# Row maxima in a rotation of three PSUM banks, one output accumulator for the first image, and a new order within a step

## The chip, the cores and the metric

One core of a Trainium2 chip runs the whole kernel. The metric is the device time in microseconds (us); lower is better. The engines are called as the profile calls them: PE (TensorE, its matmuls; PEld its weight loads), DVE (VectorE), ACT (ScalarE), POOL (GpSimd), SP (the engine that issues most DMAs).

## What is computed

The input is two images `x [2, 128, 32, 32]` in float32. Cut to what matters here, the reference does:

```python
# layer 0, per image: group norm, then 4-head attention over the 1024 pixels
qkv = einsum('bchw,oc->bohw', group_norm(x), qkv_weight)      # head_dim 32
attn = softmax(einsum('bnchw,bncyx->bnhwyx', q, k) / sqrt(C)) # 1024 x 1024 per head
x = einsum('bchw,oc->bohw', einsum('bnhwyx,bncyx->bnchw', attn, v), out_weight) + out_bias + x
# layer 1, on tokens [2, 1024, 128]
t = t + linear_attention(layer_norm(t))          # 8 heads, softmax of keys over the tokens
t = t + top2_of_8_experts(layer_norm(t))         # router, gelu MLP 128 -> 512 -> 128
```

The change is in the softmax attention of layer 0. Its softmax is taken with the true row maximum, so the kernel computes every score twice: once with queries on partitions, to get the maximum of each row, and once transposed (keys on partitions), with the maximum folded into the matmul as two more rows of the contraction, to be exponentiated and multiplied with the values.

## The kernel before

**Tiling.** The attention is cut into 4 units (`UNITS`, u): image u // 2, head pair u % 2. A unit has 16 steps (`STEPS`): two halves of the queries (512 each) by 8 key tiles of 128 (`KT`). That makes 64 steps s. A step's `scores` are two matmuls (one per head, L845) into the banks 2, 3 or 4, 5, alternating by step; ACT exponentiates both at once into `probs` (`exps`, L558); `values` (L864) multiplies with the values and with ones, four products that run beside each other in the four column groups of the array, each issued as two passes, eight matmul instructions a step. They accumulate in bank 6 or 7 (`bank(6 + o % 2)`), where o counts the eight query halves of all units; the accumulator of one o is complete after 8 steps. DVE then closes it: `norm_sums` (a transpose of the row sums), `norm_reciprocal`, `norm_product`, which writes `attn` and frees the bank (`o_used`).

**Row maxima.** One "slot" g is the maximum of 128 query rows of one head over all 1024 keys. Up to g = 7 these are plain. Every later pair slot is "folded": with K1, K2 the two halves of the keys, max(qK1, qK2) = qK2 + relu(q(K1 - K2)). So `max_first(g)` (L806) writes q(K1 - K2) into bank 1, ACT applies relu into the SBUF buffer `above` (`max_above`, L551, two buffers), `max_second(g)` (L826) writes qK2 into bank 0, and DVE adds the two and takes the maximum in one instruction (`max_slot`, L1189). After 8 slots of a group k, DVE makes two columns `mhl` of the 16 maxima; a "rows" slot turns them on PE (L821), DVE copies them to `mrow` (L1181), and SP sends them by DMA into the score operands `Qs` (`max_rows`, L352). `scores` of the first step of a query half waits for that DMA (`mrow_in[k]`). The slots are handed out ahead of the scores: `new_slots(s)` gives steps 0 to 31 two slots each (steps 15 and 31 one); the rows slots fall on steps 5, 9, 14, 19, 23, 28 and 31. From step 33 on, the layer 1 work of the first image is run between `scores` and `values` of the steps of the second image; t_centre, t_residual and t_project are its first parts.

**Order of the work.** Each engine's program is written out by hand and run in order. Before the change PE does in step s: `max_first` of the first new slot, `scores` of step s + 1, `max_second` of the first slot, `max_first` of the second slot, layer 1 parts, `values` of step s, `max_second` of the second slot. ACT does: exp of step s, relu of the second slot of step s - 1, layer 1 parts, relu of the first slot of step s.

**What waits for what.** `max_first` waits until ACT has read bank 1 (`above_ready`); `max_second` until DVE has read bank 0 (`slot_used`); `values` of step s until exp(s) is done; the first `values` of an accumulator until DVE has used up the one before it in the same bank.

**POOL.** After the loads of `Kd` (the stacked K1 - K2) POOL waits for `mrow_in[0]` and issues two DMAs of 1.5 MB that zero the expert input in HBM (L478).

Of the kernel before, what the change touches and what calls it, by code (L numbers as in the profile page):

```python
# [6 lines left out]
def build_program(nc, x, gn_weight, gn_bias, qkv_weight, out_weight, out_bias, Wk, bk, Wq, bq, Wv, bv, Wr, br,  # L7
# [44 lines left out]
    with ctx:  # L52
# [91 lines left out]

        gst = sb("gst", [P, B, 2, 6])
# [65 lines left out]
        st_ready, exp_done, pv_done, o_used = sem("st_ready"), sem("exp_done"), sem("pv_done"), sem("o_used")  # L211
        proj_ready, t_sb, F_ready = sem("proj_ready"), sem("t_sb"), sem("F_ready")
# [20 lines left out]

        SP_LOADS = 2
        GN_BANK = (3, 1)
        QV_BANK = ((0, 0), (2, 4))
# [32 lines left out]
        def before_in(g, slots):  # L269
            return max((x for x in slots if x < g and slot_banks(x) == slot_banks(g)), default=None)  # L270
# [131 lines left out]
        def _(pool):  # L402
# [72 lines left out]
            pool.wait_ge(mrow_in[0], 16 * 2)  # L475
# [35 lines left out]
        def _(act):  # L511
# [32 lines left out]
            def max_above(g):  # L544

                if g in nth_folded:
                    n = nth_folded[g]
                    act.wait_ge(diff_ready, n + 1)
                    if n >= 2:
                        act.wait_ge(slot_used, folded[n - 2] + 1)  # L550
                    nc.scalar.activation(above[:, n % 2, :], bank(slot_banks(g)[1]), ACT.Relu).then_inc(above_ready, 1)  # L551

            def exps(u, step):
# [4 lines left out]
                nc.scalar.activation(probs[:, s % 3, :], bank(2 + 2 * (s % 2), 2), ACT.Exp).then_inc(exp_done, 1)  # L558

# [74 lines left out]
            for s in range(UNITS * STEPS):  # L634
                exps(s // STEPS, s % STEPS)
                if s:
                    for g in new_slots(s - 1)[1:]:
                        max_above(g)
                run_parts(layer1, LAYER1_AT, s, 0)
                for g in new_slots(s)[0:1]:  # L640
                    max_above(g)
# [59 lines left out]
        def _(pe):  # L701
# [80 lines left out]

            def max_first(g):
# [11 lines left out]
                before = before_in(g, pairs)  # L795
                if before in nth_folded:
                    pe.wait_ge(above_ready, nth_folded[before] + 1)
                else:
                    pe.wait_ge(slot_used, before + 1)
# [3 lines left out]
                if g in nth_folded:  # L803
                    if g == folded[0] or u != order[folded[nth_folded[g] - 1]][0] // 2:
                        pe.wait_ge(kd_in[u], 16 * 6)
                    nc.tensor.matmul(bank(slot_banks(g)[1]), q, Kd[0:SPLIT, b, n, :], start=True,  # L806
                                     stop=True).then_inc(diff_ready, 1)
                else:
# [707 lines left out]
```

## Time and profile before

| | us |
|---|---|
| Time, median of 3 runs | 363.89 (363.23 to 364.35) |
| Span of the profiled execution | 384.2 |
| PE busy | 334.2 (87%) |
| ACT busy | 204.4 (53%) |
| DVE busy | 202.1 (53%) |
| POOL busy | 110.8 (29%) |
| `values` (L864), 512 matmul instructions in two groups of 256 | 68.2 each group |
| exp (L558) x64 | 65.3 |
| DVE maximum of folded slots (L1189) x56 | 38.7 |
| relu (L551) x56 | 33.5 |
| `max_second` (L826) x56 | 28.0 |
| `max_first` (L806) x56 | 23.4 |

How to read it: the span is the time from the first to the last instruction of one profiled execution; it is longer than the timed runs, and no other time of that execution is given. Busy times are sums over the whole span and mix stages with different limits, so the views of the chain, the waits and the timeline below are by stretch. A busy PE is not a PE at its peak: the times of matmuls overlap, and a matmul's length holds its pipeline's end. The granted clock is given in tenths of 2.4 GHz; 0.50 is the lower level of 1.2 GHz.

### The profile page before, as it was taken

Reading aid. Unit: us, or ns where it says so; the run is one execution under the profiler, and the core shown is the slowest. Engines: PE = TensorE matmul, PEld = TensorE weight load, DVE = VectorE, ACT = ScalarE, POOL = GpSimd, SP = SyncE. Lnnn points to the kernel's source line nnn. Section 1 sums busy time; section 2 is a strip of 40 time slices with the busy share of each in tenths; the row PEclk is TensorE's granted clock in tenths of the full one; section 3 lists DMA queues with packets and bytes.
Section 4 is the critical chain, followed back from the end, with each engine's and each line's share of the span. In section 5 each row is a group of like instructions: output and inputs, shape, how many; then the busy total and the mean of one; then the engine's idle time right before and its main releaser. Section 6 shows DMA issues by size and latency. Waiting matters only on the chain.

```text
span 384.2 us, 6582 instructions
## 1 busy us (share of the span) xinstructions
PE 334.2 (87%) x2004; PEld 211.5 (55%) x2004; DVE 202.1 (53%) x616; ACT 204.4 (53%) x324; POOL 110.8 (29%) x140
## 2 busy tenths in 40 slices
PE   7879799899999989999998496967551999999996
PEld 3533343333333335445432354867551999999996
DVE  2584444563756553565576248666402455777620
ACT  1460765666576554655585023665212677777732
POOL 2082291000000001000307630061774344444430
PEclk9985989999999999999999879996665899999999
DMA  6078768660000025000001102010211222222415
GB/s 186 2 149 194 170 146 333 154 243 34 0 2 3 3 72 149 0 2 1 2 0 43 55 8 62 16 28 23 62 62 34 64 72 70 71 66 79 143 37 210
DMA packets 21772, 29.28 MB, mean 76 GB/s; under 512 B 4055, under 2 KB 15628, under 8 KB 21484
## 3 DMA queue, kind: packets, MB, share of 16 engines
q1 hardware_dynamic: 16808, 18.04, 17.7%
q0 software_dynamic: 3744, 10.31, 8.4%
q10 hardware_dynamic: 1188, 0.53, 0.6%
q8 instruction: 17, 0.28, 0.3%
q14 instruction: 15, 0.12, 0.1%
HBM read 11.62 MB, written 9.25 MB: 54 GB/s over the span
## 4 chain that ended last, share of the span: by engine, by line
PE 70%; DVE 13%; issue 6%; another core or an unknown queue 4%; ACT 3%; DMA 1%; POOL 1%; DVEq 0%; SPq 0%; ACTq 0%; POOLq 0%
PE ps L864 15%; PE ps L1081 10%; PE ps L1068 9%; PE ps L845 6%; PE ps L826 6%; DVE above L1189 4%; PE ps L706 2%; PE ps L806 2%; PE ps L922 2%; PE ps L746 2%; PE ps L899 2%; PE ps L778 1%; PE ps L891 1%; DMA Qs<-mrow 1%
## 5 line engine op out<-in xcount | busy, mean ns | idle before, releaser
L558 ACT ACTIVATE probs<-ps 128x1024 f32<-128x1024 f32 x64 | 65.3, 1021 | 37.0 <-PE ps L845 36.9
L1081 PE MATMUL ps<-w,GT 128*128 x368 | 55.0, 297 | 18.8 <-ACT GT L684 15.0
L864 PE MATMUL ps<-probs,vT 128*32 128x512 f32 x256 | 68.2, 608 | 1.1 <-ACT probs L558 1.1
L864 PE MATMUL ps<-probs,ones 128*32 128x512 f32 x256 | 68.2, 609 | 0.0
L1081 PEld LDWEIGHTS ps<-w,GT 128*128 128x128 f32 x368 | 49.3, 208 | 22.0 <-issue 21.7
L1189 DVE CUSTOM_DVE_ANT_0 above<-ps,above 128x512 f32<-128x512 f32 x56 | 38.7, 691 | 40.8 <-PE ps L826 39.0
L496 POOL DMA_INDIRECT token_out<-Y,yidx x46 | 44.2, 961 | 48.2 <-DVE Y L1480 46.6
L433 POOL TENSOR_TENSOR rstd<-ve,minus_half 128x1 f32<-128x1 f32 (+2 forms) x6 | 10.3, 1724 | 160.6 <-DVE ve L1231 88.6
L1068 PE MATMUL ps<-XTT,w1s 128*128 128x128 f32 x368 | 53.1, 291 | 3.2 <-issue 3.2
L684 ACT ACTIVATE GT<-H 128x512 f32<-128x512 f32 x46 | 28.9, 629 | 46.5 <-DVE H L1469 27.4
L1068 PEld LDWEIGHTS ps<-XTT,w1s 128*128 128x128 f32 x368 | 49.2, 208 | 4.3 <-issue 4.3
L551 ACT ACTIVATE above<-ps 128x512 f32<-128x512 f32 x56 | 33.5, 599 | 25.3 <-PE ps L806 25.3
L1469 DVE TENSOR_TENSOR H<-ps,b1T 128x512 f32<-128x512 f32 x46 | 31.8, 691 | 27.8 <-PE ps L1068 7.4
L845 PE MATMUL ps<-Qs,Ks 98*128 98x512 f32 x128 | 44.0, 425 | 1.8 <-DMA Qs<-mrow 1.1
L845 PEld LDWEIGHTS ps<-Qs,Ks 98*128 98x128 f32 x128 | 21.8, 191 | 31.0 <-issue 23.7
L491 POOL DMA_INDIRECT expert_in<-X,slots x32 | 31.0, 969 | 25.4 <-DVE slots L1374 16.3
L826 PEld LDWEIGHTS ps<-Ks,Qs 96*128 96x128 f32 x56 | 10.6, 190 | 38.1 <-DVE pm L1189 32.8
L826 PE MATMUL ps<-Ks,Qs 96*128 96x512 f32 x56 | 28.0, 500 | 3.5 <-DVE pm L1189 1.4
L659 ACT ACTIVATE w1s<-w 128x512 f32 x46 | 28.5, 619 | 0.5 <-issue 0.4
L1480 DVE TENSOR_TENSOR Y<-ps,bias 128x128 f32<-128x128 f32 x46 | 13.3, 290 | 23.3 <-remote 11.1
L666 ACT ACTIVATE XTT<-ps,affine 128x128 f32<-128x128 f32 x46 | 20.3, 442 | 9.5 <-PE ps L1042 9.5
L806 PE MATMUL ps<-Kd,Qs 96*128 96x512 f32 x56 | 23.4, 418 | 1.0 <-ACT above L551 1.0
(196 smaller groups left out, 427.5 us busy)
## 6 DMA issues: line engine op xcount, KB each, us to landing
expert_in<-zeros POOLq DMA_DIRECT2D x2, 1495.0 KB, 7.6
XR<-expert_in SPq DMA_DIRECT2D x46, 65.0 KB
Qs<-q_hi SPq DMA_DIRECT2D x16, 128.0 KB, 3.1
w<-in_L_ffn_W SPq DMA_DIRECT2D x1, 2048.0 KB, 8.4
w<-in_L_ffn_W SPq DMA_DIRECT2D x8, 256.0 KB, 4.1
YG<-token_out SPq DMA_DIRECT2D x8, 256.0 KB, 4.1
Ks<-k_hi SPq DMA_DIRECT2D x14, 128.0 KB, 2.6
X<-in_x SPq DMA_DIRECT2D x2, 512.0 KB, 4.6
```

The costliest lines, as they stand in the source:

```text
L491: pool.indirect_dma_start(xs[:, :], bass.IndirectOffsetOnAxis(ap=slots[:, b, w, j:j + 1], axis=0), X2[:, b, j, :], None).then_inc(scattere ...
L496: pool.indirect_dma_start(yt[:, :], bass.IndirectOffsetOnAxis(ap=yidx[:, t:t + 1], axis=0), Y[:, t % NBY, :], None).then_inc(y_sent[t % NB ...
L551: nc.scalar.activation(above[:, n % 2, :], bank(slot_banks(g)[1]), ACT.Relu).then_inc(above_ready, 1)
L558: nc.scalar.activation(probs[:, s % 3, :], bank(2 + 2 * (s % 2), 2), ACT.Exp).then_inc(exp_done, 1)
L806: nc.tensor.matmul(bank(slot_banks(g)[1]), q, Kd[0:SPLIT, b, n, :], start=True, stop=True).then_inc(diff_ready, 1)
L826: last = nc.tensor.matmul(o, Qs[0:SPLIT, b, n, t * P:(t + 1) * P], Ks[0:SPLIT, b, n, HALF:L], start=True, stop=True)
L845: last = nc.tensor.matmul(bank(2 + 2 * (s % 2) + hd), Ks[0:STACK, b, n, kt * P:(kt + 1) * P], Qs[0:STACK, b, n, qh * HALF:(qh + 1) * HALF] ...
L864: last = nc.tensor.matmul(bank(6 + o % 2)[i * HD:(i + 1) * HD, :], w, probs[:, s % 3, hd * HALF:(hd + 1) * HALF], start=kt == 0, stop=kt = ...
L1068: last = nc.tensor.matmul(bank(2 + s % 2)[:, c * P:(c + 1) * P], w1s[:, s % 2, c, :], XTT[:, s % NB, :], start=True, stop=True)
L1081: last = nc.tensor.matmul(bank(4 + p)[:, 0:D], GT[:, p, c, :], w2[:, e, c, :], start=c == 0, stop=c == HC - 1)
L1189: nc.vector.tensor_tensor_reduce(above[:, n % 2, :], bank(base), above[:, n % 2, :], scale=1.0, scalar=-3.0e38, op0=ALU.add, op1=ALU.max, ...
L1469: nc.vector.tensor_tensor(H1[:, s % NB, :].rearrange("p (c t) -> p c t", c=HC), bank(2 + s % 2).rearrange("p (c t) -> p c t", c=HC), b1T[: ...
```

## The change

- `max_first` and `max_second` no longer use the fixed banks 1 and 0, but take the next of the three banks 1, 0, 7 in turn (`RING_BANKS`), in the order in which PE issues them; each use waits for the reader of the use three before it (`wait_bank`): DVE's `slot_used` after a `max_second` or a rows slot, ACT's `above_ready` after a `max_first`. The first use of bank 7 waits for `slot_used >= 10`.
- Bank 7 comes from the accumulators. For o = 0 to 3 (the first image) there is one accumulator, bank 6. When it is complete, ACT copies its 128 x 512 values into the new SBUF tile `acc` (`acc_copy`, after the exp of the steps 8, 16, 24 and 32); the next accumulator's first `values` waits for that copy, and DVE closes o from `acc`. From o = 4 on, banks 6 and 7 alternate as before.
- PE's order in a step: `max_first` of the first slot, `scores(s + 1)`, `max_first` of the second, `max_second` of the first, `max_second` of the second, layer 1 parts, `values(s)`.
- ACT's order: exp(s), then `acc_copy` if due, then the relus of both slots of step s, then layer 1 parts.
- POOL waits for `mrow_in[1]` in place of `mrow_in[0]` before the DMAs that zero the expert input.

```diff
@@ -142,6 +142,7 @@
 
+        acc = sb("acc", [P, HALF])
         gst = sb("gst", [P, B, 2, 6])
@@ -209,6 +210,7 @@
         st_ready, exp_done, pv_done, o_used = sem("st_ready"), sem("exp_done"), sem("pv_done"), sem("o_used")
+        acc_copied = sem("acc_copied")
         proj_ready, t_sb, F_ready = sem("proj_ready"), sem("t_sb"), sem("F_ready")
@@ -231,8 +233,13 @@
 
+        def acc_bank(o):
+            return ACC if o < COPIED else ACC + o % 2
+
         SP_LOADS = 2
         GN_BANK = (3, 1)
+        ACC = 6
+        COPIED = UNITS
         QV_BANK = ((0, 0), (2, 4))
@@ -266,8 +273,24 @@
 
-        def before_in(g, slots):
-            return max((x for x in slots if x < g and slot_banks(x) == slot_banks(g)), default=None)
+        RING_BANKS = (1, 0, 7)
+        uses = [(g, half) for g in range(PLAIN_FIRST + 1, AHEAD) for half in (0, 1)]
+        for s in range(2 * STEPS):
+            new = new_slots(s)
+            uses += [(g, 0) for g in new[0:2]] + [(g, 1) for g in new[0:2]] + [(g, half) for g in new[2:] for half in (0, 1)]
+        uses = [(g, half) for g, half in uses if half or order[g][1] != "rows"]
+        nth_use = {use: n for n, use in enumerate(uses)}
+
+        def ring_bank(g, half):
+            return RING_BANKS[nth_use[g, half] % len(RING_BANKS)]
+
+        def base_bank(g):
+            return ring_bank(g, 1) if (g, 1) in nth_use else slot_banks(g)[0]
+
+        def use_before(g, half):
+
+            n = nth_use[g, half]
+            return uses[n - len(RING_BANKS)] if n >= len(RING_BANKS) else None
 
@@ -472,7 +495,7 @@
                                 allow_small_or_imprecise_dtypes=True))
-            pool.wait_ge(mrow_in[0], 16 * 2)
+            pool.wait_ge(mrow_in[1], 16 * 2)
             for b in range(B):
@@ -548,7 +571,7 @@
                         act.wait_ge(slot_used, folded[n - 2] + 1)
-                    nc.scalar.activation(above[:, n % 2, :], bank(slot_banks(g)[1]), ACT.Relu).then_inc(above_ready, 1)
+                    nc.scalar.activation(above[:, n % 2, :], bank(ring_bank(g, 0)), ACT.Relu).then_inc(above_ready, 1)
 
@@ -556,6 +579,13 @@
                 nc.scalar.activation(probs[:, s % 3, :], bank(2 + 2 * (s % 2), 2), ACT.Exp).then_inc(exp_done, 1)
+
+            def acc_copy(o):
+
+                act.wait_ge(pv_done, KT * (o + 1))
+                if o:
+                    act.wait_ge(o_used, o)
+                nc.scalar.activation(acc[:, :], bank(ACC), ACT.Copy).then_inc(acc_copied, 1)
 
@@ -633,12 +663,11 @@
                 exps(s // STEPS, s % STEPS)
-                if s:
-                    for g in new_slots(s - 1)[1:]:
-                        max_above(g)
+                if s % KT == 0 and 0 < s <= KT * COPIED:
+                    acc_copy(s // KT - 1)
+                for g in new_slots(s):
+                    max_above(g)
                 run_parts(layer1, LAYER1_AT, s, 0)
-                for g in new_slots(s)[0:1]:
-                    max_above(g)
             run_parts(layer1, LAYER1_ACT, "before", 1)
@@ -780,6 +809,16 @@
 
+            def wait_bank(g, half):
+
+                before = use_before(g, half)
+                if before is None:
+                    pe.wait_ge(slot_used, AHEAD if ring_bank(g, half) == 7 else PLAIN_FIRST)
+                elif before[1]:
+                    pe.wait_ge(slot_used, before[0] + 1)
+                else:
+                    pe.wait_ge(above_ready, nth_folded[before[0]] + 1)
+
             def max_first(g):
@@ -792,30 +831,23 @@
                         pe.wait_ge(stack_in[u], 16 * 12)
-                before = before_in(g, pairs)
-                if before in nth_folded:
-                    pe.wait_ge(above_ready, nth_folded[before] + 1)
-                else:
-                    pe.wait_ge(slot_used, before + 1)
+                wait_bank(g, 0)
                 hd, t = i // QH, QH * qh + i % QH
...
                 q = Qs[0:SPLIT, b, n, t * P:(t + 1) * P]
-                if g in nth_folded:
-                    if g == folded[0] or u != order[folded[nth_folded[g] - 1]][0] // 2:
-                        pe.wait_ge(kd_in[u], 16 * 6)
-                    nc.tensor.matmul(bank(slot_banks(g)[1]), q, Kd[0:SPLIT, b, n, :], start=True,
-                                     stop=True).then_inc(diff_ready, 1)
-                else:
-                    nc.tensor.matmul(bank(slot_banks(g)[1]), q, Ks[0:SPLIT, b, n, 0:HALF], start=True, stop=True)
+                if g == folded[0] or u != order[folded[nth_folded[g] - 1]][0] // 2:
+                    pe.wait_ge(kd_in[u], 16 * 6)
+                nc.tensor.matmul(bank(ring_bank(g, 0)), q, Kd[0:SPLIT, b, n, :], start=True, stop=True).then_inc(diff_ready, 1)
 
...
                 b = u // PAIRS
-                before = before_in(g, range(SLOTS))
-                if before is not None:
-                    pe.wait_ge(slot_used, before + 1)
-                o = bank(slot_banks(g)[0])
+                if (g, 1) in nth_use:
+                    wait_bank(g, 1)
+                else:
+                    pe.wait_ge(slot_used, g - 1)
+                o = bank(base_bank(g))
                 if i == "rows":
@@ -855,13 +887,17 @@
                     if kt == 0:
-                        if o >= 2:
+                        if o == 0:
+                            pe.wait_ge(slot_used, AHEAD)
+                        elif o <= COPIED:
+                            pe.wait_ge(acc_copied, o)
+                        elif o == COPIED + 1:
+                            pe.wait_ge(slot_used, SLOTS)
+                        else:
                             pe.wait_ge(o_used, o - 1)
-                        else:
-                            pe.wait_ge(slot_used, AHEAD)
                 n = head(u, hd)
                 for i, w in ((hd, vT[:, b, kt, n * HD:(n + 1) * HD]), (2 + hd, ones[:, 0:HD])):
-                    last = nc.tensor.matmul(bank(6 + o % 2)[i * HD:(i + 1) * HD, :], w,
+                    last = nc.tensor.matmul(bank(acc_bank(o))[i * HD:(i + 1) * HD, :], w,
                                             probs[:, s % 3, hd * HALF:(hd + 1) * HALF],
@@ -1014,18 +1050,16 @@
                         scores((s + 1) // STEPS, (s + 1) % STEPS, hd)
-                for g in new[0:1]:
-                    max_second(g)
                 for g in new[1:2]:
                     max_first(g)
+                for g in new[0:2]:
+                    max_second(g)
                 if s == BEGIN_LAYER1:
...
                     values(s // STEPS, s % STEPS, hd)
-                for g in new[1:2]:
-                    max_second(g)
                 for g in new[2:]:
@@ -1173,7 +1207,7 @@
                 k, i = order[g]
-                base, other = slot_banks(g)
+                base = base_bank(g)
                 dve.wait_ge(slot_ready, g + 1)
@@ -1199,11 +1233,17 @@
 
+            def closed(o):
+                return acc if o < COPIED else bank(acc_bank(o))
+
             def norm_sums(o):
-                dve.wait_ge(pv_done, (o + 1) * KT)
+                if o < COPIED:
+                    dve.wait_ge(acc_copied, o + 1)
+                else:
+                    dve.wait_ge(pv_done, (o + 1) * KT)
                 if o:
                     dve.wait_ge(o_used, o)
-                link(nc.vector.transpose(sums[:, :], bank(6 + o % 2)[64:128, :]))
+                link(nc.vector.transpose(sums[:, :], closed(o)[64:128, :]))
 
@@ -1214,7 +1254,7 @@
                 place = attn[64 * pair:64 * pair + 64, b, :].rearrange("c (j p) -> c p j", j=J)[:, qh * 64:(qh + 1) * 64, :]
-                nc.vector.tensor_tensor(place, bank(6 + o % 2)[0:64, :].rearrange("c (p j) -> c p j", j=J),
+                nc.vector.tensor_tensor(place, closed(o)[0:64, :].rearrange("c (p j) -> c p j", j=J),
                                         rec[:, :].rearrange("c (p j) -> c p j", j=J), ALU.mult).then_inc(o_used, 1)
```

## Rows read from the trace of the kernel before

**Rows 1.** Chain that ended last, 46 to 165 us: start, us, what.

```profile
53.99 0.99 PE ps L864 x8
55.45 0.69 DVE above L1189
...
138.91 1.04 PE ps L864 x8
...
143.13 2.02 PE ps L884 x16
...
150.26 0.99 PE ps L864 x8
...
151.92 0.99 PE ps L864 x8
```

**Rows 2.** Who waited for whom, 46 to 144 us: us in total, times, longest.

```profile
PEld ps L826 <- DVE pm L1189: 31.5, 45, 1.0
```

**Rows 3.** Timeline of one step: start, us, engine, line, operation [idle before, releaser].

```profile
54.91 0.50 PE L826 MATMUL ps<-Ks,Qs 96*128 96x512 f32 x1
55.25 0.39 PE L806 MATMUL ps<-Kd,Qs 96*128 96x512 f32 x1
55.48 0.62 PE L845 MATMUL ps<-Qs,Ks 98*128 98x512 f32 x2
56.21 0.50 PE L826 MATMUL ps<-Ks,Qs 96*128 96x512 f32 x1
56.55 0.40 PE L806 MATMUL ps<-Kd,Qs 96*128 96x512 f32 x1
56.88 0.62 PE L864 MATMUL ps<-probs,vT 128*32 128x512 f32 x1
...
57.87 0.50 PE L826 MATMUL ps<-Ks,Qs 96*128 96x512 f32 x1
```

**Rows 4.** The same step on ACT, and the weight load that follows the relu.

```profile
55.68 0.60 ACT L551 ACTIVATE above<-ps 128x512 f32<-128x512 f32 x1 [0.94 <-PE ps L806]
56.17 1.02 ACT L558 ACTIVATE probs<-ps 128x1024 f32<-128x1024 f32 x1
57.08 0.60 ACT L551 ACTIVATE above<-ps 128x512 f32<-128x512 f32 x1
...
56.35 0.19 PEld L806 LDWEIGHTS ps<-Kd,Qs 96*128 96x128 f32 x1
```

**Rows 5.** Timeline on PE: the start of the steps, and values of the steps 0, 1, 31.

```profile
44.93 0.49 PE L826 MATMUL ps<-Ks,Qs 96*128 96x512 f32 x1 [0.86 <-DVE pm L1189]
...
46.82 0.65 PE L864 MATMUL ps<-probs,vT 128*32 128x512 f32 x1
...
50.97 0.62 PE L864 MATMUL ps<-probs,vT 128*32 128x512 f32 x1
...
138.84 0.62 PE L864 MATMUL ps<-probs,vT 128*32 128x512 f32 x1
```

**Rows 6.** Granted clock: 40 slices of the span, then one microsecond (clock third from last).

```profile
PEclk9985989999999999999999879996665899999999
...
48.00:49.00 1.00, 1.00 (x6) 0.62 (x3) 0.00 (x0) 0.00 (x0) 1.00 (x3) 0.50 1.02 201
```

**Rows 7.** Chain and timeline at the second row maxima; page's DMA issues (us to landing).

```profile
62.73 0.66 SPq L352
63.44 4.85 DMA Qs<-mrow
...
58.12 1.15 POOL L478 DMA_DIRECT2D expert_in<-zeros  x2 [0.32 <-POOL zeros L473]
...
Ks<-k_hi SPq DMA_DIRECT2D x14, 128.0 KB, 2.6
```

**Rows 8.** DVE's last closing of the first image: its first instruction and the one behind it.

```profile
139.97 0.72 DVE L1206 STREAM_TRANSPOSE rec<-ps 64x512 f32<-64x512 f32 x1 [0.75 <-PE ps L864]
...
142.82 0.17 DVE L1247 SCALAR_TENSOR_TENSOR rw<-ps,rw 128x8 f32<-128x8 f32 x1
```

## The prediction

> **What bounds the kernel now.** I read the chain that ended last first, because it says which engine sets the end at each time. From about 50 to 139 us it alternates between PE's `values` and DVE's maximum of a folded slot; from 150 us on it is PE alone, with `values` every 1.66 us [rows 1]. So the first 32 steps are the only part of the attention in which PE is held up. The view of waits says by what: the weight load of `max_second` stood 31.5 us in 45 waits, for DVE to finish its maximum [rows 2]. That is not 31.5 us of loss, since the load merely stands ready while matmuls run; the timeline of one step gives the loss [rows 3]. The step lasts from 54.91 to 57.87, 2.96 us, and closes on itself: second slot's `max_second` at 54.91, its result read by DVE from 55.45 [rows 1] for 0.70, then the next `max_second` in the same bank 0 at 56.21, `max_first` at 56.55, `values` at 56.88, and after 0.99 the next `max_second`. 0.54 + 0.76 + 0.34 + 0.33 + 0.99 = 2.96. PE's matmuls need less. In steps without slots it takes 1.66 [rows 1], and a slot matmul costs 0.23 when nothing holds it (55.25 to 55.48) [rows 3]: 1.66 + 4 x 0.23 = 2.58. The loss is 0.38 us a step.
>
> **The rotation and the new order** are one edit for the cost. Let V be the end of `values`. PE then issues `max_first` a at V (its record 0.50 long, like the one at 54.91), scores at V + 0.34, `max_first` b at V + 0.79, `max_second` a at 1.02, b at 1.25, `values` at 1.58, done at 2.57: the floor of 2.58, by the spacings of [rows 3]. Now the waits. Counting three uses back, `max_first` a waits for the relu of the last step's b; `max_first` b for DVE on the last step's a; `max_second` a for DVE on the last step's b; `max_second` b for the relu of this step's a. DVE takes 0.70 a slot (0.69 in [rows 1] and the handoff): a from V + 1.45 to 2.15, b to 2.9, which is 0.3 into the next step, where 1.02 is early enough. ScalarE: relu a at V + 0.53 to 1.13, relu b from 1.22, exp(s + 1) 0.49 behind it (56.17 against 55.68) to 2.73 [rows 4]. Everything PE needs of exp is a step old by then, as `values` comes late. Queued behind the now later exp are the copy and the relus of the next step; the next relu can be issued 0.91 after an exp (57.08 against 56.17) [rows 4], so at V + 2.62, and is wanted at 3.1. The one wait that can bite is `max_second` b behind relu a: relu end 1.13, weight load 0.07 later, matmul 0.20 after that (56.28, 56.35, 56.55) [rows 3, 4] makes 1.40 in place of 1.25. In that row the 0.20 coincides with the ordinary spacing, so a part of it may not be a cost. Bounds 2.58 and 2.73; I take the middle, 2.66.
>
> Between the starts of `values(0)`, 46.82, and `values(31)`, 138.84, lie 92.02 us and 31 steps [rows 5]. In the new order: 22 steps with two pair slots, 22 x 2.66 = 58.5; six with a pair and a rows slot, 1.66 + 2 x 0.23 + 0.15 for the small transpose (0.15 is an estimate, bounded by nothing and one slot matmul's 0.23) = 2.27, together 13.6; step 15 with one pair, 2.12; step 31, rows alone, 1.66 + 0.15 and an estimated 0.25 until DVE has `mhl`, 2.06. Sum without the first step 76.3.
>
> **The start.** The first use of bank 7 waits for slot 9's maximum on DVE, which releases PE at 44.93 [rows 5]; scores of step 1 queue behind it. The matmuls that lay on both sides of that wait then run in one piece, and I get `values(0)` at 46.92, 0.1 later. The first step took 4.15 [rows 5], as the granted clock was 0.50 [rows 6], the 1.2 GHz level, after PE had idled; I keep the clock and take out 0.25 of waiting: 3.9.
>
> **The second row maxima.** Step 8's scores wait for a DMA: issued from 62.73, landed at 68.29 [rows 7], about 1.1 us too late. In that time 3 MB of zeros, issued at 58.12, go out. The change puts the zeros behind that DMA. New times: rows copied at 61.2, scores wanted at 65.05. With the old 5.56 from issue to landing it lands at 66.8 and stalls 1.7; by the nearest row of a load that is not behind the zeros, 2.6 us to landing [rows 7] after two issues of 0.66, it is in time. I take 0.3, nearer to the second, as what was in the way is gone. The zeros themselves are next needed after 144 us; SP's stack loads, which they now meet, serve slots from step 23 on.
>
> **Copies and closings.** `acc_copy` has the shape of the relu, 0.60 us [rows 4]; either end of its cost is near, nothing to 0.6 for each of three. exp(s) is over at V + 0.1, `values(s - 1)` too, and relu a is wanted at 0.53, so the copy lies in ScalarE's gap and delays the relu by 0.06. DVE closes o from `acc`; I keep the durations that it has from PSUM. A closing adds about 2.9 us to DVE over two steps of which it uses 1.4 each, so it runs over by under 0.3; 0.15 for each of three closings, 0.45 with the copies. Bound above: the 0.6 each.
> The fourth closing is on the path: `values(31)` end, `norm_sums` from 139.97, reciprocal, product, rw at 142.82 [rows 8], then t_residual at 143.13 [rows 1]. The copy now stands in front of it: 0.60 more.
>
> **Sum.** 76.3 + 3.9 + 0.1 + 0.3 + 0.45 = 81.05 against 92.02: 11.0 gained, less 0.6: 10.4 us. From 143 us on PE is the chain and each wait depends on the work before it, so it is carried to the end: a span of 384.2 - 10.4 = 373.8. The median of the timed runs, 363.89, is 20.3 below the span; I take the gain as it is in microseconds, since the steps are short of nothing that profiling adds to: 353.5.
>
> **Rivals.** (B) A new wait takes the place of the old one: `max_second` b always waits the full time for relu a, 2.73 a step, and the row maxima still land late. 22 x 0.07 + 1.4 = 2.9 less: 356.4. For it: the handoff is in the rows. (C) Neither bites, 2.58 a step: 22 x 0.08 = 1.8 more, 351.7. (D) Slower: the clock. PE idles a little longer in one piece before 44.93 and does more in bursts; if the granted clock then stays at 0.50 over steps of the stage, each costs 2 x 2.58 - 2.66 = 2.5 more. From 4.2 such steps on it is slower than before; with five, 366.0. Against: before the change, with a gap in every step, the slices of this stage stand at 9 [rows 6]. The Trainium skill (TensorE: Matmul & The Clock Gate, on PSUM-queue depth-cycling) warns of just this: PE idling in small gaps between groups that rotate through banks can make the clock swing. The trace has the gaps and not the swing here; by that rule the sum would be D's. (E) The change doesn't do what it says: the banks were not what held the step, it stays at 2.96, and only the late DMA's 1.1 is gained and the copy's 0.6 lost: 363.4.
>
> **Chances.** Forecast 0.62, B 0.20, C 0.08, D 0.05, E 0.03, the rest (0.02) slower by something unseen. The range reaches from beyond C to beyond B, for the waits of 6 to 11 us between 212 and 300 us may shift by a microsecond: 350.5 to 358.5. A measurement of this kernel tells 0.3%, 1.1 us, from no change. Faster 0.90, same 0.03, slower 0.07.
>
> **What would show it.** `values` about every 2.66 us in plain steps, and the wait of L826 for DVE gone from the chain; no or a small wait on `Qs<-mrow` before 70 us; DVE's `norm_sums` in the fourth closing some 0.6 later behind `values(31)`; the clock at 9 between 52 and 133 us. Steps at 2.9, or a clock at 5 there, would make the prediction wrong.

## The result and the profile after

| | before | after |
|---|---|---|
| Time, median of 4 runs each, us | 363.56 (361.95 to 364.35) | 353.30 (352.02 to 356.14) |
| Ratio, with 95% interval | | 0.9735 (0.9698 to 0.9771) |
| Span of the profiled execution, us | 384.2 | 351.4 |
| `values(0)` to `values(31)`, us | 92.0 | 80.0 |
| `values(31)` to the first t_residual, us | 4.29 | 4.90 |

The forecast was 353.5 in a range of 350.5 to 358.5: faster by 10.4 us, measured 10.3 by the medians and 9.6 (8.3 to 11.0) by the ratio. The two spans differ by 32.8 us, three times as much. That is no effect of the change: a second profile of the kernel before has a span of 361.1 (below).

The page of the changed kernel; the first line is the span, then busy time by engine, the granted clock in 40 slices, and the groups that answer to the table ahead of the prediction (L900 is `values`, L581 exp, L1223 DVE's maximum, L574 relu, L840 `max_first`, L858 `max_second`):

```profile
span 351.4 us, 6589 instructions
...
PE 321.8 (92%) x2004; PEld 207.9 (59%) x2004; DVE 201.8 (57%) x616; ACT 208.8 (59%) x328; POOL 110.7 (31%) x140
...
PEclk9996989999999999999999998698969999999999
...
L581 ACT ACTIVATE probs<-ps 128x1024 f32<-128x1024 f32 x64 | 65.3, 1020 | 27.7 <-PE ps L877 27.6
L900 PE MATMUL ps<-probs,vT 128*32 128x512 f32 x256 | 68.5, 610 | 0.3
...
L1223 DVE CUSTOM_DVE_ANT_0 above<-ps,above 128x512 f32<-128x512 f32 x56 | 37.2, 689 | 29.8 <-PE ps L858 28.3
...
L574 ACT ACTIVATE above<-ps 128x512 f32<-128x512 f32 x56 | 33.4, 597 | 17.7 <-PE ps L840 14.9
...
L840 PE MATMUL ps<-Kd,Qs 96*128 96x512 f32 x56 | 25.4, 453 | 1.6 <-DVE pm L1223 1.6
```

The work is the same: exp, relu and `values` to 0.3 us, and a maximum on DVE takes 689 ns where it took 691; the copies are new, four of 0.6 us. (That `max_first` shows 2.0 more, and `max_second` 20.0 in place of 28.0, is no other work: the records of matmuls overlap, and how far depends on their order.) What went is waiting. Between 44 and 134 us the view of waits shows for `max_second` (L858) and `max_first` (L840):

```profile
PEld ps L840 <- ACT above L574: 17.6, 21, 0.8
...
PEld ps L858 <- ACT above L574: 3.6, 18, 0.3
...
PEld ps L858 <- DVE pm L1223: 2.2, 4, 0.8
```

This answers to the 31.5 us of [rows 2]: what `max_second` waits for now is mostly the relu, by 0.3 us at most, and DVE four times, by up to 0.8. The 17.6 us of `max_first` are a weight load that stands ready while `values` runs; they don't hold the step, as its start right behind `values` shows. A plain step on PE, the counterpart of [rows 3]:

```profile
50.35 0.50 PE L840 MATMUL ps<-Kd,Qs 96*128 96x512 f32 x1
50.68 0.64 PE L877 MATMUL ps<-Qs,Ks 98*128 98x512 f32 x2
51.16 0.40 PE L840 MATMUL ps<-Kd,Qs 96*128 96x512 f32 x1
51.40 0.64 PE L858 MATMUL ps<-Ks,Qs 96*128 96x512 f32 x2
51.97 0.62 PE L900 MATMUL ps<-probs,vT 128*32 128x512 f32 x1
...
52.96 0.50 PE L840 MATMUL ps<-Kd,Qs 96*128 96x512 f32 x1
```

50.35 to 52.96 is 2.61 us, where 54.91 to 57.87 was 2.96. The starts of `values`, read from the timeline for all steps, give the whole stage. Here and below, a measured step k is the time from the start of `values(k - 1)` to that of `values(k)`:

| steps | predicted us each | measured | |
|---|---|---|---|
| plain, two pairs | 2.66 | 2.61 to 2.62 | 15 of them |
| 8, 16, 24 (copy) | | 2.69 to 2.70 | |
| 4 | | 3.18 | not foreseen |
| 18; 26 and 27 (closings) | | 3.16; 2.74 and 2.81 | 0.87 above plain, together |
| six with a rows slot | 2.27 | 2.22 to 2.25 | |
| 15; 31 | 2.12; 2.06 | 2.11; 1.92 | |
| 1 (first, at the lower clock) | 3.9 | 3.33, 3.66 in a second profile | |

### The profile page after: what moved, and what is told of

It is laid out like the page before. It is cut to its first block, busy times and chain, and to the rows that moved or that the text cites. A ratio compares the mean times of both kernels' runs of the same rounds, so it can differ in the third digit from the quotient of the medians.

```text
span 351.4 us, 6589 instructions
## 1 busy us (share of the span) xinstructions
PE 321.8 (92%) x2004; PEld 207.9 (59%) x2004; DVE 201.8 (57%) x616; ACT 208.8 (59%) x328; POOL 110.7 (31%) x140
## 4 chain that ended last, share of the span: by engine, by line
PE 78%; DVE 10%; POOL 5%; issue 4%; ACT 2%; DVEq 0%; POOLq 0%
PE ps L900 15%; PE ps L1115 12%; PE ps L1102 12%; PE ps L877 9%; PE ps L840 5%; PE ps L858 4%; POOL expert_in L514 4%; PE ps L958 3%; PE ps L735 2%; PE ps L807 2%; PE ps L775 2%; PE ps L1076 1%; DVE pm L1226 1%; PE ps L973 1%; PE ps L1142 1%
## 5 line engine op out<-in xcount | busy, mean ns | idle before, releaser
L581 ACT ACTIVATE probs<-ps 128x1024 f32<-128x1024 f32 x64 | 65.3, 1020 | 27.7 <-PE ps L877 27.6
L900 PE MATMUL ps<-probs,vT 128*32 128x512 f32 x256 | 68.5, 610 | 0.3
L900 PE MATMUL ps<-probs,ones 128*32 128x512 f32 x256 | 68.5, 611 | 0.0
L1115 PE MATMUL ps<-w,GT 128*128 x368 | 51.9, 286 | 5.7 <-ACT GT L713 5.5
L1102 PE MATMUL ps<-XTT,w1s 128*128 128x128 f32 x368 | 51.7, 286 | 4.9 <-issue 4.9
L1223 DVE CUSTOM_DVE_ANT_0 above<-ps,above 128x512 f32<-128x512 f32 x56 | 37.2, 689 | 29.8 <-PE ps L858 28.3
L456 POOL TENSOR_TENSOR rstd<-ve,minus_half 128x1 f32<-128x1 f32 (+2 forms) x6 | 10.4, 1725 | 136.2 <-DVE ve L1271 61.0
L1102 PEld LDWEIGHTS ps<-XTT,w1s 128*128 128x128 f32 x368 | 47.5, 202 | 6.1 <-issue 6.1
L1115 PEld LDWEIGHTS ps<-w,GT 128*128 128x128 f32 x368 | 46.8, 199 | 7.2 <-issue 7.0
L574 ACT ACTIVATE above<-ps 128x512 f32<-128x512 f32 x56 | 33.4, 597 | 17.7 <-PE ps L840 14.9
L840 PE MATMUL ps<-Kd,Qs 96*128 96x512 f32 x56 | 25.4, 453 | 1.6 <-DVE pm L1223 1.6
L840 PEld LDWEIGHTS ps<-Kd,Qs 96*128 96x128 f32 x56 | 10.6, 190 | 25.8 <-ACT above L574 17.6
L900 PEld LDWEIGHTS ps<-probs,vT 128*32 128x32 f32 x256 | 9.8, 108 | 19.9 <-issue 16.7
L858 PE MATMUL ps<-Ks,Qs 96*128 96x512 f32 x56 | 20.0, 428 | 0.6 <-DVE pm L1223 0.6
## 6 DMA issues: line engine op xcount, KB each, us to landing
expert_in<-zeros POOLq DMA_DIRECT2D x2, 1495.0 KB, 10.3
```

The source lines that it names most:

```text
L574: nc.scalar.activation(above[:, n % 2, :], bank(ring_bank(g, 0)), ACT.Relu).then_inc(above_ready, 1)
L840: nc.tensor.matmul(bank(ring_bank(g, 0)), q, Kd[0:SPLIT, b, n, :], start=True, stop=True).then_inc(diff_ready, 1)
L858: last = nc.tensor.matmul(o, Qs[0:SPLIT, b, n, t * P:(t + 1) * P], Ks[0:SPLIT, b, n, HALF:L], start=True, stop=True)
L900: last = nc.tensor.matmul(bank(acc_bank(o))[i * HD:(i + 1) * HD, :], w, probs[:, s % 3, hd * HALF:(hd + 1) * HALF], start=kt == 0, stop=kt ...
L1102: last = nc.tensor.matmul(bank(2 + s % 2)[:, c * P:(c + 1) * P], w1s[:, s % 2, c, :], XTT[:, s % NB, :], start=True, stop=True)
L1115: last = nc.tensor.matmul(bank(4 + p)[:, 0:D], GT[:, p, c, :], w2[:, e, c, :], start=c == 0, stop=c == HC - 1)
```

## The experiments

Two measures are used. The time is the median of the timed runs, with the ratio to the kernel before from the same chip. The stage is the time from `values(2)` to `values(31)` in the profile, since the first two steps depend on where the clock falls (step 1 alone took 2.62 to 4.72 in the profiles of kernels with the rotation). "Behind" is what is left of the span after `values(31)`, and "low" the part of it in which the granted clock stood at 0.50, without the last microseconds of the span. Times of different groups of runs were taken on different chips, so the ratios are what compares.

| kernel | time, us | ratio (95%) | stage, us | behind, us | low, us |
|---|---|---|---|---|---|
| before, second profile | 362.89, one run | | 84.84 | 223.5 | 17.1 |
| before, zeros late | 362.86 | 0.9993 (0.9975 to 1.0011) | 83.85 | 223.3 | 17.1 |
| new order, two banks | 404.33, two runs | 1.1126 (1.1077 to 1.1174) | 116.33 | 224.8 | 20.5 |
| rotation, old order | 353.38 | 0.9749 (0.9709 to 0.9790) | 76.43 | 222.8 | 13.7 |
| after | 353.30 | 0.9735 (0.9698 to 0.9771) | 74.05 | 225.4 | 20.5 |
| after, again | 353.22 | 0.9716 (0.9688 to 0.9744) | 74.07 | 225.8 | 20.5 |
| after, zeros early | 357.06 | 0.9819 (0.9788 to 0.9851) | 79.54 | 222.5 | 17.1 |
| after, no fourth copy | 351.97 | 0.9687 (0.9663 to 0.9712) | 73.51 | 224.9 | 20.5 |
| the same, bank 7 earlier | 352.71 | 0.9715 (0.9679 to 0.9750) | 73.76 | 223.3 | 17.1 |
| after, memset late | 352.37 | 0.9701 (0.9666 to 0.9735) | 73.49 | 223.7 | 17.1 |
| after, closing spread | 351.86, one run | | 72.92 | 223.9 | 17.1 |
| after, copy twice | 354.23, one run | | 77.27 | 223.0 | 13.7 |
| three edits together | 349.64 | 0.9642 (0.9609 to 0.9675) | 72.60 | 222.9 | 17.1 |

**The kernel before, profiled again.** No edit.

> The kernel before, unchanged, profiled once more. Theory: the span of 384.2 us ahead of the prediction is that of one execution which lost about 20 us behind 212 us (waits of 6 and 11 us near 276 and 283 us that the profile puts down to an unknown queue), so this span is about 361.5, that is 2 us under its time, as in the changed kernel (351.4 against 353.5), and the first 32 steps take 92.0 us between values(0) and values(31) as before. Rival: profiling itself adds 20 us to this kernel; then the span is again about 384.

Measured: span 361.1 at a time of 362.89, `values(0)` to `values(31)` 91.98. So profiling doesn't add the 20 us; the execution shown ahead of the prediction had lost 21.9 us behind `values(31)` (245.4 against 223.5). Its view of waits for 205 to 300 us held them, under releasers it couldn't name:

```profile
ACT t L565 <- remote: 11.8, 1, 11.8
DVE Y L1480 <- remote: 11.1, 1, 11.1
```

What an execution of 384.2 us loses in waits of 11 us is not the kernel's. The attention stage of that profile was sound, and the sum used only that stage.

**Rotation without the new order.** PE's and ScalarE's programs as before, banks as after:

```diff
-uses += [(g, 0) for g in new[0:2]] + [(g, 1) for g in new[0:2]] + ...
+uses += [(g, half) for g in new for half in (0, 1)]
 ...
-for g in new[1:2]: max_first(g)
-for g in new[0:2]: max_second(g)
+for g in new[0:1]: max_second(g)
+for g in new[1:2]: max_first(g)
 ... layer 1 parts, values ...
+for g in new[1:2]: max_second(g)
```

> The changed kernel with the old order of PE and ScalarE in a step (rotation of three banks, copies and late zeros kept). Theory (rotation and order share the gain): the second slot's max_second still stands behind values, DVE is done with it only 1.25 us after values end, and the second max_first of the next step, three uses on, waits for that until about 1.5 in place of 1.25: steps of 2.80 to 2.85, 22 x 0.13 and 1.0 for the earlier row DMA, less 0.6 each for the start and the fourth copy: about 361. Rival (the third bank alone frees the step): steps of 2.62 and the same 353 as the whole change.

Measured: steps of 2.71 to 2.73, stage 76.43, time 353.38. The expectation of 361 was wrong. The wait that it named is there (the third line), but small:

```profile
100.17 0.50 PE L861 MATMUL ps<-Ks,Qs 96*128 96x512 f32 x1
...
101.20 0.39 PE L861 MATMUL ps<-Ks,Qs 96*128 96x512 f32 x1
101.47 0.49 PE L843 MATMUL ps<-Kd,Qs 96*128 96x512 f32 x1
101.89 0.62 PE L903 MATMUL ps<-probs,vT 128*32 128x512 f32 x1
```

`max_first` (L843) is held until 101.47, 0.03 to 0.04 us behind its place 0.23 after 101.20, and PE then needs 0.42 to `values` in place of 0.33, as its weight load isn't hidden: 0.10 a step above 2.61, where the expectation had 0.22 to 0.27 above 2.58. I had put the handoff (0.27 from the end of a reader to the matmul) where PE's record starts with the load. This kernel keeps the late zeros and the copies. Of the stage's 10.8 us the late zeros bring 1.0 (84.84 to 83.85, below), the third bank 7.4 (83.85 to 76.43) and the order 2.4, taken in this sequence; the zeros are worth more where the steps are short, as will be seen. The order's 2.4 aren't spread evenly: 1.06 is step 31 (1.92 in place of 2.98), where the last pair slot's maximum comes earlier, and 0.85 step 8 (2.70 in place of 3.55). In the time the order doesn't show at all, ratios of 0.9749 against 0.9735 and 0.9716 with intervals that overlap: the stage is 2.4 shorter with it and what lies behind is 2.6 longer. The granted clock differs there, between 190 and 290 us (after, then rotation with the old order; clock third from last):

```profile
190.00:290.00 100.00, 84.05 (x561) 69.46 (x554) 61.06 (x204) 52.90 (x95) 52.82 (x52) 0.90 0.19 53
```

```profile
190.00:290.00 100.00, 83.69 (x575) 67.74 (x574) 62.88 (x213) 54.57 (x98) 52.89 (x52) 0.93 0.19 53
```

**The new order on two banks.** The kernel before with PE's and ScalarE's new order.

> The kernel before with only the new order of PE and ScalarE, on the two fixed banks. Theory: the second max_first waits within its step for the first relu (1.40 us behind the end of values), and the second max_second for DVE's maximum of the first slot, at about 3.0; steps of about 4.3 us, 22 x 1.35 = 30 us slower: about 390 to 395. Rival (the order brings the gain and the bank is a detail): under 363.

Measured: 404.33, plain steps of 4.12 to 4.16, 11% slower. The steps are near the 4.3 expected; what comes on top are steps at the lower clock: 1 to 3 and 29 and 30 at 5.3 to 6.1 us, and 18 at 5.4. In steps 18, 29 and 30 nothing but the idle time of every step went before: PE idles 0.22 and 0.79 us in a plain step, never for more than 0.9 at once between 64 and 159 us, and the clock, at 1.00 for most of that time, fell twice (clock third from last):

```profile
118.00:122.00 4.00, 4.00 (x13) 1.40 (x14) 2.57 (x7) 1.01 (x2) 0.00 (x0) 0.57 0.00 0
...
159.00:173.00 14.00, 12.78 (x39) 4.26 (x38) 3.07 (x9) 4.22 (x6) 0.00 (x0) 0.51 0.01 2
```

Both waits stand within the step, as expected (the second `max_first` for the relu, `max_second` for DVE):

```profile
101.82 0.50 PE L803 MATMUL ps<-Kd,Qs 96*128 96x512 f32 x1
...
103.01 0.50 PE L803 MATMUL ps<-Kd,Qs 96*128 96x512 f32 x1 [0.22 <-ACT above L551]
...
104.53 0.50 PE L823 MATMUL ps<-Ks,Qs 96*128 96x512 f32 x1 [0.79 <-DVE pm L1184]
```

The order alone is a loss of 41 us. It is worth something only where the rotation stands under it.

**The zeros.** One line in either kernel, `pool.wait_ge(mrow_in[0], ...)` against `mrow_in[1]`.

> The kernel before with only POOL's wait changed, so that the zeros go out behind the second row maxima's DMA. Theory: step 8's scores no longer wait for that DMA: the step that took 3.97 takes 2.95, 1.0 us less, ratio 0.997. Rival (the DMA's time is its own, the zeros don't matter): same time, the wait on Qs<-mrow stays.

> The changed kernel with the zeros sent out as before, behind the first row maxima. Theory A (as in the prediction's rival B): the DMA of the second row maxima again takes 5.6 us from its issue at about 60.2 and lands at 65.8, and the scores want it at 66.5, so nothing is lost: same time. Theory B: the steps that are now faster want it earlier than it comes: up to 1.7 us slower, a wait on Qs<-mrow in the trace.

Measured. In the kernel before, step 7 falls from 3.97 (3.89 in the second profile) to 2.95 and the stage by 1.0, as expected; the time doesn't show it (0.9993), so whether it is carried to the end is open. In the changed kernel the same line is worth 5.5 us of the stage and 3.8 of the time, more than either theory had. Of the stage's 5.5, 4.0 is step 7 and 1.7 step 8, less 0.2 in step 4. The late row maxima held the scores, and the clock fell behind the gap. Chain, timeline and windows of the kernel with early zeros:

```profile
61.89 5.87 DMA Qs<-mrow
```

```profile
64.62 0.51 PE L840 MATMUL ps<-Kd,Qs 96*128 96x512 f32 x1
67.80 1.22 PE L877 MATMUL ps<-Qs,Ks 98*128 98x512 f32 x2 [2.68 <-DMA Qs<-mrow]
```

```profile
67.00:71.00 4.00, 3.20 (x9) 1.70 (x13) 1.08 (x3) 1.51 (x2) 0.29 (x2) 0.53 0.71 165
```

The row DMA, issued at 61.18, lands at 67.76, 6.6 us later; the second of its two issues takes SP 1.22 us in place of 0.65. PE idles 2.68 us, and the granted clock is then 0.53 over four microseconds, near the 1.2 GHz level: step 7 takes 6.61 and step 8 4.35, where the changed kernel has 2.61 and 2.69. With the zeros behind it the same DMA lands 2.5 us after its first issue. That shows best in the kernel with the late memset (below), where POOL's memset begins as soon as the DMA has landed, issued at 59.97, landed at 62.47:

```profile
59.97 1.35 SPq L375 DMA_DIRECT2D Qs<-mrow  x2
```

```profile
62.47 2.60 POOL L496 MEMSET zeros<- 128x2990 f32 x1 [8.73 <-DMA Qs<-mrow]
```

**The changed kernel again.** No edit.

> The changed kernel, unchanged, in more rounds and with a second profile. Theory: 353.3 again; 80.0 us between values(0) and values(31), or 79.4 if the 1.02 us that one tiny operation on mhl took at 55 us (0.17 elsewhere), which held step 4, was an accident of one execution. The time behind values(31), 225.4 in the first profile and 222.8 in the kernel with the old order, goes with the granted clock between 200 and 280 us: executions with a higher mean clock are the shorter ones. Rival: the new order itself costs the 2.6 us behind values(31); then they stay at any clock.

Measured: 353.22; stage 74.07; step 4 again long, 3.15. It was no accident. Over its six runs the time goes roughly with the mean granted clock: 352.02 to 353.38 at 0.961, 354.51 at 0.956, 354.36 at 0.952; in the four runs of the result, 353.49 at 0.956 and 356.14 at 0.947. The mean clock isn't all of it: nine runs of the kernel before with late zeros took 361.70 to 364.08 at the same 0.957.

The rival, that the new order itself costs the 2.6 us behind `values(31)`, is settled by the other profiles of the table: they have the same order, and behind `values(31)` 222.5 to 223.9 us where the clock was low for 13.7 or 17.1 us, against 224.9 to 225.8 where it was low for 20.5. The kernel with the new order on two banks, low for 20.5, has 224.8. An estimate from these columns: 3.4 us more at half the clock cost 1.7 us if PE sets the pace, and the changed kernel's 225.4 is 1.7 above the 223.7 of the one with the late memset. With that, and 0.6 for each copy on the path more or less, the column "behind" comes out to within 0.8 us in all but one kernel; with early zeros it is 1.2 shorter, and why is open. Mean clock over 130 to 345 us, after, memset late, rotation with the old order:

```profile
130.00:345.00 215.00, 197.47 (x1408) 150.73 (x1409) 126.87 (x430) 123.77 (x211) 84.23 (x82) 0.95 0.20 57
...
130.00:345.00 215.00, 197.70 (x1425) 151.40 (x1426) 126.57 (x430) 124.36 (x213) 84.24 (x82) 0.96 0.20 57
...
130.00:345.00 215.00, 196.74 (x1424) 149.34 (x1424) 128.77 (x433) 125.31 (x214) 84.33 (x82) 0.97 0.21 59
```

Why one execution meets one clock pattern and the next another wasn't found, so differences of 1 to 2 us between medians here hold a part that is not the edit's.

**The memset.** In step 3 the first operation on `mhl` took 1.02 us, elsewhere 0.17, and ended with POOL's memset (53.58 + 2.59 = 56.17 against 55.17 + 1.02 = 56.19). DVE and POOL of the changed kernel:

```profile
55.17 1.02 DVE L1232 TENSOR_SCALAR mhl<-pm 128x8 fp32r<-128x8 f32 x1
```

```profile
53.58 2.59 POOL L495 MEMSET zeros<- 128x2990 f32 x1
```

The experiment moves the wait ahead of the memset:

```diff
+pool.wait_ge(mrow_in[1], 16 * 2)
 link(nc.gpsimd.memset(zeros[:, :, :], 0.0))
 link(nc.gpsimd.iota(zeros[:, :, D], ...))
-pool.wait_ge(mrow_in[1], 16 * 2)
```

> The changed kernel with POOL's memset of the zeros also behind its wait for the second row maxima. In three profiles (53.58 + 2.59, and twice more) DVE's first operation on mhl of step 3 ended within 0.03 us of the end of that memset, and took 0.76 to 1.02 us in place of 0.17; where the two did not overlap it took 0.17. Theory: DVE's operation is held by the memset; with the memset moved step 4 takes 2.61 in place of 3.17, 0.57 less between values(0) and values(31) beside the first two steps. Rival (something else that is there at 55 us, the DMAs or the operation's place): step 4 stays at about 3.17.

Measured: the operation takes 0.17, step 4 takes 2.61, the stage falls by 0.57 to 73.49. A stronger case came unasked in the kernel with two copies, whose execution reached that point earlier against POOL; the operation on 8 columns stood for 2.31 us, to the memset's end (54.90 + 2.59 = 57.49, 55.21 + 2.31 = 57.52), and step 4 took 4.49:

```profile
55.21 2.31 DVE L1235 TENSOR_SCALAR mhl<-pm 128x8 fp32r<-128x8 f32 x1
```

```profile
54.90 2.59 POOL L496 MEMSET zeros<- 128x2990 f32 x1
```

DVE's maxima, with one operand in PSUM, run through the same memset at 0.69. In the kernel before the operation began at 57.48, 0.06 ahead of the memset's end (54.95 + 2.59 = 57.54), and took 0.17. The Trainium skill (SBUF — State Buffer, Who interferes with whom) says that VectorE in its two-port modes, which `tensor_scalar` can enter, shares a port pair with GpSimd under an exclusive lock, and that the one that comes second blocks fully; the trace agrees in that the memset came first and the operation waited to its end. That this operation was in such a mode no run shows.

**The closings.** DVE's transpose, reciprocal and product in three steps in place of two, each behind both maxima:

```diff
-product = s % KT == 2 and KT < s < BEGIN_LAYER1
-for g in new[0:1]: max_slot(g)
+product = s % KT == 3 and KT < s < BEGIN_LAYER1
+reciprocal = (s % KT == 2 and KT < s < BEGIN_LAYER1) or (closing and not phase_a)
+for g in new[0:2]: max_slot(g)
 if closing: norm_sums(o)
-for g in new[1:2]: max_slot(g)
-if closing: norm_reciprocal()
+if reciprocal: norm_reciprocal()
```

> The changed kernel with DVE's closing of an accumulator spread over three steps and behind both maxima: transpose in the first, reciprocal in the second, product in the third. Theory: the steps 17, 25 and 26 (3.17, 2.74, 2.82) are long because the transpose stands ahead of the second maximum and the product ahead of the next; all three take 2.61 to 2.65, 0.8 less. Rival (DVE is over-full in any order): the excess only moves to the steps behind.

Measured: the three steps, which the expectation numbers by DVE's work (17, 25 and 26) and which are 18, 26 and 27 by the starts of `values`, take 2.61, 2.61 and 2.62. Stage 72.92; of the difference to 74.05, 0.25 is step 4 (2.93) and 0.88 the closings. What they had run into in the changed kernel behind `values(17)`, on DVE:

```profile
90.16 0.69 DVE L1223 CUSTOM_DVE_ANT_0 above<-ps,above 128x512 f32<-128x512 f32 x1 [1.40 <-PE ps L858]
...
90.89 0.17 DVE L1232 TENSOR_SCALAR mhl<-pm 128x8 fp32r<-128x8 f32 x1
91.10 0.17 DVE L1233 SCALAR_TENSOR_TENSOR mhl<-pm,mhl 128x8 fp32r<-128x8 f32 x1
91.30 0.71 DVE L1246 STREAM_TRANSPOSE rec<-acc 64x512 f32<-64x512 f32 x1
92.04 0.69 DVE L1223 CUSTOM_DVE_ANT_0 above<-ps,above 128x512 f32<-128x512 f32 x1
```

The `mhl` operations and the transpose, 1.15 us, stand between the two maxima, so the next step's `max_second` waits for the second, to 92.80.

**The copies.** Every copy twice (`activation(acc, bank(ACC), Copy)`, wait, and once more).

> The changed kernel with every copy of the accumulator made twice, one behind the other. Theory: the copy lies in ScalarE's gap ahead of the first relu and costs 0.08 (steps 8, 16, 24 take 2.69 to 2.71 in place of 2.62) because the gap is only just long enough; a second copy has none, so these steps grow by about 0.6 more to 3.2 to 3.3, and values(31) to t_residual by 0.6 to 5.5. Rival (ScalarE has slack, the 0.08 is from something else): these steps stay at 2.7.

Measured: steps 8, 16, 24 take 3.33, `values(31)` to t_residual 5.53 (2.50 and 4.98 for the steps 32 and 33 against 1.87 and 4.98, so 0.63 more). One copy costs 0.08, the next 0.63: the gap holds just one.

**No fourth copy.** The last accumulator of the first image is closed in bank 6, the second image begins in bank 7:

```diff
-return ACC if o < COPIED else ACC + o % 2
+return ACC if o < UNITS else ACC + 1 - o % 2
-COPIED = UNITS
+COPIED = UNITS - 1
```

and the fillers go to bank 7.

> The changed kernel without the fourth copy: the last accumulator of the first image is closed in its bank 6, and the second image begins in bank 7. Theory: from values(31) to t_residual 4.25 us in place of 4.85, 0.6 us less in the end, ratio to the kernel before lower by 0.0017. Rival (PE or the wait for the last slot hides it): the same 4.85.

Measured: the steps 32 and 33 take 6.23 in place of 6.85, 0.62 less. The time is 1.25 below that of the changed kernel of the same chip, with intervals that overlap. (Its step 4 took 2.62, as its `mhl` operation fell at 57.47, behind the memset.)

**Bank 7 earlier.** With that, `pe.wait_ge(kb_sb, B)` in place of `slot_used >= 10` ahead of bank 7's first use.

> As the kernel without the fourth copy, and the first use of bank 7 waits for ScalarE's last read of that bank instead of for slot 9's maximum. Theory: the matmuls before values(0) run from about 1.2 us earlier, scores(0) to values(0) takes 4.2 in place of 4.7 and the granted clock falls later or not at all: 0.5 to 1.2 us less than the one without the fourth copy. Rival (ScalarE's exp and relu set values(0), and the clock falls all the same): no difference.

Measured: `max_first` of slot 10 starts at 42.69, not 44.23, but `values(0)` follows scores(0) by 4.14 in place of 4.44, and the clock is at 0.50 from 47 to 49 us all the same. 352.71 against 351.97, with intervals that overlap: no gain shown. ScalarE sets this point:

```profile
45.48 0.50 PE L858 MATMUL ps<-Ks,Qs 96*128 96x512 f32 x1 [0.96 <-ACT above L574]
```

**Three edits together**: no fourth copy, late memset, spread closings.

> The changed kernel with three edits: no fourth copy, the memset behind the wait, the closing spread. Theory: 0.3 (fourth copy, by the steps 32 and 33), 0.57 and 0.8 add up to 1.7 to 2.0 us: about 351.4, ratio to the kernel before 0.967. Rival (the time behind the first 32 steps, which goes with the clock, swallows it): 353.

Measured: 349.64, ratio 0.9642 (0.9609 to 0.9675), below the changed kernel's two intervals. The stage is 72.60; 74.05 - 0.57 - 0.88 is 72.60. With the 0.61 behind it the edits account for 2.1 us, and the ratios differ by 2.7 to 3.4 us. The clock can hold the rest: in this profile step 1 took 2.62 with no fall of the clock ahead of it, where the changed kernel had 3.33 and 3.66, and the clock was low for 17.1 us behind, not 20.5. Its chain at the end of the first image has no copy (the changed kernel's, then this one's):

```profile
126.09 1.04 PE ps L900 x8
127.15 0.61 ACT acc L588
127.78 0.72 DVE rec L1246
...
130.92 2.02 PE ps L920 x16
```

```profile
124.65 1.04 PE ps L900 x8
125.72 0.73 DVE rec L1246
...
128.87 2.02 PE ps L920 x16
```

## Why the prediction was right

Step by step:

- **The bound.** The loop of [rows 3] was what held the step: with the bank out of it the step is 2.61, and the floor of 2.58 by PE's spacings was 0.03 off. The middle of 2.58 and 2.73 was too careful. The wait for the relu was no cost: in the step shown relu a ends 1.13 behind `values`, as forecast, the weight load of `max_second` b starts 0.05 later, and its matmul only 0.10 after that, where I had 0.20; it stands 0.23 behind the matmul before it, which is PE's own spacing. Over the 22 steps with two pair slots 2.66 in place of 2.61 to 2.62 is about 1 us that the sum had too much.
- **The order and the rotation as one edit.** Taking them apart shows that most of the gain is the rotation's, 7.4 of 10.8 us of the stage, with 1.0 from the late zeros, and that the order adds 2.4 there. The prediction didn't say this and didn't need it.
- **Copies.** Right in kind (they lie in ScalarE's gap), 0.08 each measured against 0.06. The sum's "0.45 with the copies" is only the three closings of 0.15; the copies' 3 x 0.06 were left out of it. Closings and copies together measured 1.1.
- **Closings.** Mis-sized: 0.15 each, 0.45 in all, against 0.88; the first of the three cost nothing (step 10 takes 2.62). I had counted DVE's load over two steps and not the order in it: what counts is that a 0.7 us operation stands ahead of the second maximum, on which the next step's `max_second` waits.
- **The memset.** Not foreseen: 0.57. In the kernel before the two overlapped by 0.06 us; the faster steps moved the operation 0.9 us earlier against the memset (1.60 us behind its start in place of 2.53).
- **The row DMA.** 0.3 allowed, nothing measured, and 2.5 us from the first issue to landing, in time as I had it from the nearest row, and faster than that row. Rival B's price for the other side, 1.7, was far too low: with the zeros early it is 5.5 in the stage, for the DMA took 6.6 in place of 5.6 and the clock fell behind the gap, a cost that the sum for B had not.
- **Fourth copy on the path.** 0.60 forecast, 0.61 measured (4.90 against 4.29) and 0.62 by taking it out.
- **The start.** scores(0) to `values(0)` took 4.71 and 4.45 against 4.15; I had 0.1 more. The first step took 3.33 and 3.66 against the 3.9 forecast. Together near.
- **Carried to the end.** 12.0 less 0.6 left the stage; 10.3 arrived. 1.3 to 1.7 us more than the copy were lost behind `values(31)` (225.4 and 225.8 against 223.5 in the kernel before). The clock was low there for 20.5 us in both, for 17.1 in the kernel before, and by the estimate above that is about all of the loss; what made it low more often is open. So two errors met: the steps gave 1 us more than forecast, and the rest gave a part back. That 10.3 lies so near 10.4 is luck in part; that it lies in the range is not.
- **Profile against time.** I read 20.3 us as what profiling adds. It was one disturbed execution. The gain in microseconds was right since it was worked out in a stage that the disturbance hadn't touched.
- **Rival D, the clock.** Over the rotating banks it stood at 1.00 from 58 to 126 us. The warning of the Trainium skill (TensorE: Matmul & The Clock Gate, PSUM-queue depth-cycling) isn't borne out by the rotation: in none of its ten profiles did the clock fall between 58 us and `values(31)`, but for the 2.68 us of idle time with early zeros. But gaps alone can do it: with the new order on two banks, where PE idles 0.22 and 0.79 us in every plain step, the clock fell at 118 and at 159 us with no idle time over 0.9 before it. What rival D feared is there in the kernel without the third bank.

## What to carry to other kernels

Write down the loop that closes a step, reader by reader, and compare its length with the engine's own spacing: the difference times the steps is what another buffer gives, and here one more bank gave most of it without any reordering, and the reordering without the bank cost 41 us. When the steps get faster, look at everything that was timed against them: a DMA that was 1 us late became worth 5.5 us of the stage, a memset on another engine moved into a VectorE operation, and a gap held one copy but not two. A shorter stage can't be judged by the time alone while the clock behind it varies by 2 us; the starts of one instruction in all steps tell to a hundredth.

## What the runs showed of the hardware

- A POOL memset of 2.59 us holds a VectorE `TENSOR_SCALAR` from SBUF to SBUF until it ends: 2.31 and 1.02 us in place of 0.17, while VectorE operations that read PSUM pass at 0.69.
- Two DMAs of 4 KB each took 2.5 us from the first issue to landing with the queues all but idle, and 5.5 to 6.6 us with 3 MB of zeros in flight from another queue; of that, SP's second issue took 1.22 us in place of 0.65.
- One idle time of PE of 2.68 us was followed by a clock of 0.53 over four microseconds. Gaps of 0.10 to 0.34 us in some twenty steps of the kernel before, and one of 1.12 us (1.04 in its second profile), were not followed by a fall. Gaps of 0.22 and 0.79 in every plain step of the two-bank kernel went with a clock of 1.00 for 54 us and then a fall.
- The same idle times aren't always followed by the same clock: 0.69 and 1.56 us at 41 to 44 us were followed by a fall in seven of nine profiles and not in two, and step 1 of these kernels took 2.62 to 4.72 us, depending on when the clock fell and rose.
